# Multiplying probabilities by values two key tiles at a time, from a ring of ten probability tiles

## The reference, cut to what matters

```python
q = split_heads(x1 @ Wq.T); k = split_heads(mem @ Wk.T); v = split_heads(mem @ Wv.T)
scores = einsum('bhqd,bhkd->bhqk', q, k) / sqrt(16)      # 512 queries x 1601 keys per head
attn = softmax(where(mask, scores, -inf), axis=-1)
out = einsum('bhqk,bhkd->bhqd', attn, v)
# feed-forward part, per batch:
h = relu(x @ W_enc + b_enc); recon = h @ W_dec + b_dec   # for each of 8 adapters
losses = mean((recon - x) ** 2)                          # argmin picks the adapter
```

## Time and profile before

| | |
|---|---|
| median of 3 runs | 1750.64 us (1748.94 to 1752.38) |
| profiled execution | 1749.5 us, with a span of 1747.7 us |
| mean granted TensorE clock | 0.972 of full speed; full from 351 us to 1516 us |
| TensorE busy | 1634.2 us, 94% |
| VectorE busy | 1237.4 us, 71% |
| ScalarE busy | 1063.7 us, 61% |
| GpSimd busy | 160.0 us, 9% |

### The profile page before, as it was taken

The page is one execution under the profiler, slowest core; times in us unless marked ns, Lnnn a source line. Parts: engine busy times, 40 slices in busy tenths (PEclk is TensorE's granted clock), DMA queues, the critical chain, the costliest instruction groups (busy, mean ns, idle before and its releaser), DMA issues.

```text
span 1747.7 us, 25649 instructions
## 1 busy us (share of the span) xinstructions
PE 1634.2 (94%) x9787; PEld 612.5 (35%) x9787; DVE 1237.4 (71%) x1793; ACT 1063.7 (61%) x2010; POOL 160.0 (9%) x150
## 2 busy tenths in 40 slices
PE   6678989999999999999999999999999999999875
PEld 5434313233343323433334323333334334332232
DVE  4676767787778777886778777887778777777322
ACT  2114666666666666666666766666666666666640
POOL 5411000100001000110001000110001000000000
PEclk9677999999999999999999999999999999999998
DMA  5537152251607061342507070433405050600000
GB/s 152 92 81 143 36 102 54 49 89 55 106 7 136 24 121 37 74 86 64 94 3 135 25 133 26 87 73 76 83 21 120 20 85 24 108 2 2 4 25 15
DMA packets 100846, 116.58 MB, mean 67 GB/s; under 512 B 21722, under 2 KB 86107, under 8 KB 100724
## 3 DMA queue, kind: packets, MB, share of 16 engines
q1 hardware_dynamic: 97988, 113.89, 32.9%
q10 hardware_dynamic: 2736, 1.06, 0.3%
HBM read 80.12 MB, written 34.78 MB: 66 GB/s over the span
## 4 chain that ended last, share of the span: by engine, by line
PE 83%; issue 5%; ACT 5%; DVE 4%; POOL 1%; DMA 1%; ACTq 1%; POOLq 0%; DVEq 0%
PE banks L1103 22%; PE values L1122 22%; PE banks L1077 12%; PE work L987 5%; PE work L1001 5%; ACT xprobs L1254 4%; PE work L943 4%; PE work L1008 3%; PE work L1014 3%; PE work L928 3%; PE work L1017 1%; DVE xneg_max_pieces L1447 1%; PE work L993 1%; PE work L1026 1%; DVE xv_rows L1405 1%
## 5 line engine op out<-in xcount | busy, mean ns | idle before, releaser
L1254 ACT ACTIVATE xprobs<-banks 128x512 f32<-128x512 f32 x1664 | 902.4, 595 | 455.2 <-PE banks L1103 440.5
L1447 DVE TENSOR_REDUCE xneg_max_pieces<-banks 128x2 f32<-128x1024 f32 x768 | 911.1, 1220 | 285.3 <-PE banks L1077 283.1
L1103 PE MATMUL banks<-xq_stacks,xk_stacks 99*128 99x512 bf16 (+1 forms) x1664 | 523.1, 386 | 30.4 <-ACT xprobs L1254 22.7
L1122 PE MATMUL values<-xprobs,xv_rows 128*17 128x512 f32 x3328 | 438.6, 599 | 1.0 <-ACT xprobs L1254 1.0
L1103 PEld LDWEIGHTS banks<-xq_stacks,xk_stacks 99*128 99x128 bf16 (+1 forms) x1664 | 127.8, 97 | 423.5 <-ACT xprobs L1254 280.7
L1077 PE MATMUL banks<-xk_stacks,xq_stacks 49*128 49x512 bf16 (+1 forms) x2048 | 253.3, 339 | 0.8 <-DVE xneg_max_pieces L1447 0.5
L1077 PEld LDWEIGHTS banks<-xk_stacks,xq_stacks 49*128 49x128 bf16 x2048 | 56.6, 94 | 274.9 <-DVE xneg_max_pieces L1447 154.0
L1514 POOL TENSOR_TENSOR xk_parts<-xk_rest,xk_parts 128x401 bf16<-128x401 f32 (+1 forms) x64 | 59.2, 925 | 727.4 <-ACT xk_parts L1215 727.4
L1122 PEld LDWEIGHTS values<-xprobs,xv_rows 128*17 128x17 f32 x3328 | 55.1, 95 | 120.0 <-issue 118.6
L1509 POOL TENSOR_TENSOR xrstd<-xrstd,mhalf 128x4 f32<-128x4 f32 x23 | 23.2, 1010 | 661.9 <-DVE xrstd L1314 661.9
L1008 PE MATMUL work<-x2T,wenc 128*128 128x512 f32 x120 | 62.9, 608 | 0.9 <-ACT x2T L1159 0.9
(11 more groups left out here) (263 smaller groups left out, 1088.5 us busy)
## 6 DMA issues: line engine op xcount, KB each, us to landing
xk_stacks<-key_parts_dram SPq DMA_DIRECT2D x192, 200.1 KB, 11.6
key_parts_dram<-xk_parts SPq DMA_DIRECT2D x144, 100.0 KB, 1.7
xq_stacks<-parts_dram SPq DMA_DIRECT2D x186, 64.0 KB, 8.1
ctxT_a<-in_ctxT SPq DMA_DIRECT2D x4, 1601.0 KB, 7.3
ctxT_b<-in_ctxT SPq DMA_DIRECT2D x4, 1601.0 KB, 7.4
parts_dram<-xq_parts SPq DMA_DIRECT2D x45, 128.0 KB, 2.0
key_parts_dram<-xk_parts SPq DMA_DIRECT2D x48, 100.2 KB, 2.9
xa<-in_x SPq DMA_DIRECT2D x8, 512.0 KB, 14.0
```

Source lines behind the costliest of these rows:

```text
L1103: pe.matmul(scores[n % SRING], kst[0:ROWS[par], k, h2, par, t * P:(t + 1) * P], qst[0:ROWS[par], k, h2, par, :], start=True, stop=True).th ...
L1122: last = pe.matmul(av[32 * j:32 * j + HD + 1, :], vals[:, k, t, gr * GH + j, :], probs[:, sl % 2, j, :], start=t == 0, stop=t == XKT - 1)
L1254: nc.scalar.activation(probs[:, sl % 2, j, :], scores[n % SRING], ACT.Exp).then_inc(exped, 1)
L1447: nc.vector.tensor_reduce(nmp[:, of % 2, j2, :, q, piece], pairs[n % MRING][:, :, :], AX.X, ALU.max, negate=True).then_inc(on["mxr"], 1)
```

## The change

The V block is no longer in every slot. In a group, the slot t = 0 still has the block of the slot before. The odd slots have none, and the even slots from t = 2 on have two blocks in a row, of the two slots before. So 7 of the 13 slots of a group have value products, in 224 visits in place of 416; the number of products stays. The in-between job and the pairs of an odd slot directly follow its S1.

To hold probabilities longer, `probs` is one ring of ten tiles in place of two sets of four. The memory for the two extra tiles comes from `err`, which held the result of the adapter loss that nobody reads; that result is now written over its own input in the work bank. Exp no longer waits for `summed` once at a slot's start: every Exp from the eleventh on waits for the block that last read its ring tile. Two views that the self-attention at the start lays over `probs` and `err` move with them.

```diff
--- before.py
+++ after.py
@@ -33,7 +33,7 @@
 ITERS = 3
 TOK = B * HD
 EPS = 1e-5
-SRING, MRING = 2, 2
+SRING, MRING, PRING = 2, 2, 10
 NEG = -1e30
 PARTS = 3
 
@@ -726,7 +726,7 @@
         kst = sb("xk_stacks", [P, CH, HP, 2, SP_], BF16)
         qst = sb("xq_stacks", [P, CH, HP, 2, T], BF16)
         vals = sb("xv_rows", [P, CH, XKT, HC, HD + 1])
-        probs = sb("xprobs", [P, 2, GH, T])
+        probs = sb("xprobs", [P, PRING, T])
         oS = sb("xo_unnormed", [P, T])
         rz = sb("xrsum", [P, QT, GH])
         nmp = sb("xneg_max_pieces", [P, 2, GH // 2, 2, QT, WHOLE + 1])
@@ -745,7 +745,6 @@
         x2 = sb("x2", [P, QT, D])
         x2T = sb("x2T", [P, CH, T])
         hT = sb("hT", [P, NPAIR, T])
-        err = sb("err", [P, 2, T])
         loss = sb("loss", [P, NPAIR])
         lrows = sb("loss_rows", [P, 1 + CH, NE])
         xsum = sb("x2_sums", [P, CH])
@@ -1119,9 +1118,16 @@
                 elif gr == 0:
                     pe.wait_ge(on["w_free"], MAIN.order.after(("v", 7, b)))
             for j in range(GH):
-                last = pe.matmul(av[32 * j:32 * j + HD + 1, :], vals[:, k, t, gr * GH + j, :], probs[:, sl % 2, j, :],
+                last = pe.matmul(av[32 * j:32 * j + HD + 1, :], vals[:, k, t, gr * GH + j, :], probs[:, (GH * sl + j) % PRING, :],
                                  start=t == 0, stop=t == XKT - 1)
             last.then_inc(summed, 1)
+
+        def values_in(m, t):
+
+            sl = XKT * m + t
+            if t == 0:
+                return [sl - 1] if m else []
+            return [sl - 2, sl - 1] if t % 2 == 0 else []
 
         def pe_slot(m, t):
 
@@ -1130,8 +1136,8 @@
             job, part, parts = at_end(sl)
             pe_scores(m, t, 0)
             pe_scores(m, t, 1)
-            if sl:
-                pe_values(sl - 1)
+            for earlier in values_in(m, t):
+                pe_values(earlier)
             if short:
                 pe_job(MAIN, short)
             for one in pairs_at(m, t):
@@ -1250,14 +1256,14 @@
 
             sl = XKT * m + t
             n = GH * sl + j
+            if n >= PRING:
+                nc.scalar.wait_ge(summed, (n - PRING) // GH + 1)
             nc.scalar.wait_ge(made, n + 1)
-            nc.scalar.activation(probs[:, sl % 2, j, :], scores[n % SRING], ACT.Exp).then_inc(exped, 1)
+            nc.scalar.activation(probs[:, n % PRING, :], scores[n % SRING], ACT.Exp).then_inc(exped, 1)
 
         def act_slot(m, t):
 
             sl = XKT * m + t
-            if sl > 1:
-                nc.scalar.wait_ge(summed, sl - 1)
             act_exp(m, t, 0)
             act_exp(m, t, 1)
             if t == 0 and m:
@@ -1411,7 +1417,7 @@
                                   W[0:rows, 0:P].rearrange("p (h d) -> p h d", d=HD)).then_inc(on["w_free"], 1)
             elif name == "gram":
 
-                v.scalar_tensor_tensor(err[:, i % 2, :], W[:], wdb[:, i:i + 1], hT[:, i, :], ALU.add, ALU.mult,
+                v.scalar_tensor_tensor(W[:], W[:], wdb[:, i:i + 1], hT[:, i, :], ALU.add, ALU.mult,
                                        accum_out=loss[:, i:i + 1]).then_inc(on["w_free"], 1)
                 if i == NPAIR - 1:
                     v.wait_ge(on["w_free"], ph.order.after(job))
@@ -1881,10 +1887,10 @@
             "vT": [two(states[1][:, i * D:(i + 1) * D]) for i in range(ITERS)],
             "sqk": [two(squares[:, i * D:(i + 1) * D]) for i in range(ITERS)], "sqq": two(squares[:, 0:D]),
             "ksM": [hT[:].rearrange("p j t -> p (j t)").rearrange("p (c h t) -> p c h t", c=CH, h=HC)]
-                   + [probs[:, i, :, :].rearrange("p j t -> p (j t)").rearrange("p (c h t) -> p c h t", c=CH, h=HC)
+                   + [probs[:, i * GH:(i + 1) * GH, :].rearrange("p j t -> p (j t)").rearrange("p (c h t) -> p c h t", c=CH, h=HC)
                       for i in range(2)],
             "vbd": [one.rearrange("p c t -> p (c t)").rearrange("p (n k m) -> p n k m", n=PAIRS, k=QUADS)
-                    for one in (x2T[:], err[:], hT[:, 2:4, :])],
+                    for one in (x2T[:], probs[:, 2 * GH:PRING, :], hT[:, 2:4, :])],
             "rkx": wdecT[:].rearrange("p c m -> p (c m)")[:, 0:ITERS * D].rearrange("p (n h d) -> p n h d", n=ITERS, d=HD),
             "pr": oS[:], "pT": spare(1, 0, T).rearrange("p (k t) -> p k t", t=TOK),
             "m8": oS[:].bitcast(U8)[0:B, 0:S2],
```

## The result

The changed kernel takes 1796.65 us in the median (1790.59 to 1799.53, 4 runs) against 1750.4 us before. The ratio is 1.0259 (95% interval 1.0229 to 1.0289), so the change makes the kernel 46 us slower. The prediction was 1794 us, in a range of 1770 to 1814. The profiled execution took 1790.59 us, at the low end of the runs.

What follows compares the result with a forecast made beforehand. TensorE was taken to set the pace. Six inner batches at 5.99 us (35.9), batch 0 (4.0) and the last batch (5.2) sum to 45.1 us; 1749.5 + 45 gave 1794 us, range 1770 to 1814.

Steps and rivals of the forecast that it cites:

- The join of two blocks: Where one value block follows another in an even slot: 0.44 us taken, 0.43 at best, 0.53 at worst.
- the third rival: Joining two value blocks on TensorE costs the full exit: 19 us more, 1813 us, chance 8%.
- Exp late in odd slots: In plain odd slots S3' waits for the Exp of S1' until 2.92; the pair of slots costs 0.14 us more.
- Two waits ahead of every Exp: Each Exp that starts from idle starts 0.05 us late, for an extra wait instruction on ScalarE.
- The bank waits: Slots 1, 11, 35 lose 0.80 us each, 14 0.93, their transpose waiting for VectorE's subtraction; 16, 18, 27 total 1.01.
- Relief of waiting slots: Even slots where TensorE waited before gain: 0.65 us at 12, 0.33 at 10 and 49, 0.4 at 51; together 1.93.
- The sign at line 1102: TensorE's idle time before line 1102, released by Exp, grows from 23 us to some tens.
- Edits counted at nothing: The ring of ten, the loss result written over its input (3 us if all showed) and transfers cost nothing.
- First and last batch: Batch 0 becomes 4.0 us longer and the last batch 5.2 us longer.
- the drains win: Exp and bank waits stay hidden and fewer TensorE mode drains save 21 us: 1724 to 1730 us, chance 5%.
- Only Exp is late: Exp is late in odd slots but the bank waits are not: some 25 us less, 1769 us, chance 7%.
- It all cancels: Gains and losses over the whole kernel balance: 1746 to 1754 us, chance 3%.

Runs made afterwards that it cites:

- ring_only: Changed kernel with value products in every slot as before, keeping the ring of ten, two waits ahead of every Exp and the moved loss result: 1765.5 us, ratio 1.0085.
- one_wait_ref: Changed kernel with value products in every slot as before and one wait per slot, at Exp 1: 1748.3 us, ratio 0.9997.
- pair_one_wait: Changed kernel with one wait for the finished blocks per slot, at Exp 1: 1782.4 us, ratio 1.0177.
- only_bank: Changed kernel with only slots 1, 11, 14, 16, 18, 27 and 35 of every batch without their value block: 1786.4 us, ratio 1.0193.

## Why the prediction was right, step by step

- *Which slots lose their block, and the sum per slot.* Right: 192 slots, 24 of an inner batch. The sum was 5.99 us per inner batch, 5.49 were measured.
- *The price of the switch from S1 to P0*, which no row showed and I took as 0.32: 1.94 - 1.62 = 0.32. As said, it made no difference.
- *The join of two blocks* was taken as 0.44 a round. It is less: the eight products take 1.85 to the next instruction (1.87 predicted), and the even slot grows by 0.86 in place of 0.88 (slot 1 to 2, 3.88 to 4.74), that is 0.43, the bare stream. The four rounds of those products start at 857.31, 857.76, 858.19 and 858.61, and the third of them is where the second block joins. The worst case of the third rival is out. At 0.02 for 24 blocks this is 0.48 us of an inner batch. It does not explain the 0.50 by which I was high by itself, because two other errors of about that size work against each other: the relief of slots 10, 12, 49 and 51 was 0.40 larger than I said, and the four slots t = 0 became 0.24 longer together, for which my sum has no term. The Trainium skill, TensorE: Matmul & The Clock Gate, says in its section "Step-by-step: what each phase is for" (not in the one that the prediction names) that weight loads are pulled ahead of running matmuls where the row groups do not conflict or the load goes to the background weight buffer. The trace agrees: the last of the sixteen loads has ended at 858.31, and the last round of products starts at 858.61.
- *Exp late in odd slots.* S3' at 2.92 and S1'' at 4.24 were predicted; the trace has 2.92 and 4.25.
- *VectorE close behind.* P1' at 2.31 and S2' at 2.62 were predicted; it is 2.31 and 2.63.
- *Two waits ahead of every Exp.* 0.05 predicted, 0.06 measured, shown alone by ring_only against one_wait_ref and by pair_one_wait against the changed kernel. Three of the four slots t = 0 pay it too, which the sum left out.
- *The bank waits.* 0.80 for slots 1, 11 and 35, 0.93 for 14. Measured with the next slot: 0.78, 0.92 for 14, and 0.74 for 35. Slot 22 after the Relu copy, 0.51 predicted, came to 0.41, slot 37 to 0.39 (0.43 predicted), and 16, 18 and 27 to 0.42, 0.30 and 0.29 (0.39, 0.31 and 0.31). Slot 11 with 12 is only +0.06, as its relief in slot 12 belongs to it.
- *Relief of waiting slots.* 0.65 at slot 12 came as 0.71 (0.86 against 0.15), 0.33 at 10 and 49 as 0.47 (0.86 against 0.39), and 0.4 at 51 as 0.46. At 10 I had counted little more than the idle time (0.26 in the row above), not the late start in full.
- *The sign at line 1102.* I had expected TensorE's idle time before it, released by Exp, to grow from 23 us to some tens. It grew to 27.7 only. Most of the delay does not show as idle time: S3' stands 0.29 behind S2' in place of 0.22, and the rows of the two still overlap.
- *Edits counted at nothing.* Right for the ring and the loss result: one_wait_ref has both and takes 0.9997 of before.
- *First and last batch.* Here I was off, in both directions: +4.0 and +5.2 predicted, +1.1 and about +11 with the end. In the first, some 1.5 us of the difference are the slots 25 and 26 of the kernel before. In the last, 3.6 us lie behind the last S0 and 4.0 us in two slots at a lower clock, which I did not foresee (below); the rest, 3.6, is what stands against my 5.2.
- *How much of the total was luck.* By mechanism the prediction was right, and each part of its sum came out somewhat smaller than I said: 32.3 for 35.9, some 2.6 for 4.0, 3.6 for 5.2, together some 38 us for 45. That the total came within 3 us (1794 against 1796.65) is partly luck: the prediction has neither the 7.6 us of the lower clock and of the end, nor the 6 us by which the median lies above the profiled execution. My sum also started from the profiled execution (1749.5) and not from the median, which would have given 1795.7.

Of the rivals, "the drains win" is refuted in the sum, though the drain gain itself is real. "Only Exp is late" is refuted by only_bank. "It all cancels" did not happen.

## What to carry to other kernels

A block of work that seems to cost a switch may be the cover of chains that nobody sees while it is there. Before removing it, follow each wait that ends just behind it: here a two-deep ring of scores, and a single bank whose copy ended 0.14 us before its next user started. Idle time elsewhere in a slot (ScalarE's 455 us) does not help when a ring is too short to carry it over. Group such blocks only where the following slot waits anyway, and keep the extra semaphore wait on an instruction that starts behind another, not on one that starts from idle.

## What the runs showed of the hardware that was not expected

**The clock falls in the middle of a busy stretch.** The mean granted clock went from 0.972 to 0.968, and the stages of the last batch show a part of it (us, busy time and instructions of each engine, clock, transfers):

```profile
1550.00:1575.00 25.00, 23.66 (x147) 9.69 (x145) 21.83 (x34) 16.33 (x31) 1.01 (x1) 1.00 0.43 59
1575.00:1578.40 3.40, 3.40 (x17) 0.59 (x17) 1.54 (x3) 1.09 (x2) 0.00 (x0) 0.51 0.02 5
```

For 3.4 us TensorE ran at the lower of its two levels, 1.2 GHz, although it was 95% busy in the 25 us before. Just ahead stood slots 10 and 11 of the last batch, which have no end job, and slot 11 has no value products either. TensorE was idle for 0.53 us before S0 of slot 11 and again before S0 of slot 12; from 1571 to 1575 its rows cover 2.74 of 4.00 us. The fall hit the eight value products of slot 12:

```profile
1575.53 3.33 PE L1121 MATMUL values<-xprobs,xv_rows 128*17 128x512 f32 x16
```

They took 3.33 in place of 1.9. The kernel before ran its last batch at full clock up to the last S0, but it has such a stretch in batch 0, from 245.4 to 248.8, where the changed kernel has none. A second one in the changed kernel, from 1681 on, hit slot 41: these two slots are 2.4 and 2.5 us longer than before where 0.15 and 0.8 were due. That is some 4 of the 11 us of the last batch and the end. The four executions of the changed kernel have a granted clock of 0.968, 0.968, 0.964 and 0.963 for 1790.6, 1794.9, 1798.5 and 1799.5 us, so the longer ones go with the lower clock; that it is the cause of the whole spread of 9 us is not shown. The kernel before spread by 3 us in the four runs beside it, but by 10 and 11 us in the 12 and 17 runs of later series. No run here tells what exactly makes the clock fall, so that stays open.

**A second semaphore wait costs 0.06 us on ScalarE when the instruction starts from idle, and nothing when it starts behind another.** In ring_only the first Exp starts 0.49 us after its score product where it started 0.42 after it. Exp 1, which has two waits there as well, starts as soon behind Exp 0 as before (1.08 and 1.09 for the two, 1.08 before).
